# A five-stage graph network kernel: the layers' steps cut into finer pieces and listed in a new order

## The chip, the cores and the metric

The kernel runs on one core of a Trainium2 chip. The time is what the device takes for one execution, in microseconds (us). A core has five engines that run side by side and meet at semaphores: PE multiplies matrices and transposes tiles (its weight loads are shown as PEld), DVE works on vectors and reduces rows, ACT evaluates functions such as Exp and Gelu and copies, POOL does further elementwise work, and SP issues the transfers.

## What is computed

A batch of 16 graphs of 512 nodes with 128 features passes through four layers, each behind a layer norm and a ReLU.

```
h = relu(layernorm(x));  x = x + L0(h, adj)      # eight Euler steps
h = relu(layernorm(x));  x = x + L1(h, adj)      # graph attention: softmax over all neighbours, one head
h = relu(layernorm(x));  x = x + L2(h, src, dst) # attention over 256 edges, four heads
h = relu(layernorm(x));  x = x + L3(h, adj)      # Chebyshev step, 4-head masked attention, MLP
# L3: xp = L_norm @ h; x1 = relu(ln(xp @ Wc + bc)) + h
#     o = softmax(mask(q k^T / sqrt(32))) v;  x2 = ln(x1 + o @ Wo + bo)
#     out = ln(x2 + gelu(x2 @ W1 + b1) @ W2 + b2)
```

## The kernel before

The first part (`build_front`) computes layer L0 and constants; the change doesn't touch it. The second part (`build_layers`) is a software pipeline over the 16 graphs. It has five stages: `gat` (L1), `edge` (L2), `cheb` (the first half of L3 with q, k and v), `att` (the attention of L3) and `ffn` (the rest). In iteration i, stage s works on graph n = i - LAG[s], with lags of 0 to 4, so that five graphs are in flight. There are 20 iterations: 5 that fill, 11 in a hardware loop, 4 that drain.

Each engine has a list of named steps, `ORDER`, and executes it from left to right in each iteration. A step waits at semaphores for what it needs: `ready` for data, `freed` for a buffer that must have been read. An engine never goes past a waiting step, so the lists alone decide what stands behind what.

What the steps are, as far as they matter here. A node tile is 128 rows; four make a graph. Attention has 16 tiles (4 heads by 4 row tiles). In `att{j}`, PE computes the scores of tile j and transposes tile j-2 into bank c2; DVE masks tile j (L1501, `mask j` in what follows); ACT takes its Exp (L1320, `exp j`) and copies the transposed tile out of c2 (L1328). Steps att16 to att18 finish a graph in the next iteration: the last transposes (`turn 14`, `turn 15`), the row sums (`rows`) and the product with v (`pv`), which writes c2. DVE's `att_scale` (L1513) reads c2, and only then PE may transpose the next graph's tile 0 into it (`turn 0`, L1704).

In `gat`, DVE's `gat_scores` adds the mask (L1378), POOL's `gat_low` makes the scaled copy (L1247, four tiles), DVE's `gat_max` takes the larger (L1395, four tiles), ACT's `gat_exp` follows (L1288), and PE's `gat_eturn` transposes (L1597). `gat_stats` (L1110 on gat_xin) waits for `load_x` (L1181 on SP), `gat_apply` (L1145 on gat_z) for POOL's `gat_rstd`, and PE's `gat_turn` (L1558) for gat_z. In `edge`, PE's `edge_gather` (L1614, eight products of 512 columns) writes bank b0. That bank holds the product of `ffn_down` before, which DVE's `ffn_y3` (L1529) must have read. `cheb_prop` (L1664) is twelve products of 512 columns; `n1_apply` (L1145 on cheb_y) and POOL's n1 affine (L1150, L1152 on cheb_y) lead to `cheb_x1`, which PE transposes. `cheb_klow` (L1492 on k_lo) splits k. SP's `stack0` to `stack3` (L1210) move the split q and k of each head into K_parts and Q_parts with 8 transfers of 64 KB each; the scores of head h wait for `parts{h}`.

Of the kernel before, what the change touches and what calls it, by code (L numbers as in the profile page):

```python
# [1779 lines left out]
```

## Time and profile before

| what | value |
|---|---|
| time, median of 3 runs | 1535.29 us (1531.87 to 1538.79) |
| profiled execution: its own time | 1538.55 us |
| profiled execution: span, first to last instruction | 1536.8 us |
| PE busy | 1245.7 us (81%), weight loads 953.8 us (62%) |
| DVE busy | 834.5 us (54%) |
| ACT busy | 772.1 us (50%) |
| POOL busy | 471.6 us (31%) |
| mean granted clock of PE | 0.92 |

Busy time is the time in which an engine has an instruction under way. The span has three parts: L0 up to some 460 us, the pipeline's filling up to some 634 us, then the full iterations and the drain. A granted clock of 1.00 is 2.4 GHz, one of 0.50 is 1.2 GHz.

### The profile page before, as it was taken

What the parts mean: (1) busy time and instruction counts of PE and PEld (TensorE: products, weight loads), DVE (VectorE), ACT (ScalarE), POOL (GpSimd) and SP (SyncE); (2) the same over time, 40 slices, a digit from 0 to 9 for tenths busy, and PEclk for the clock granted to TensorE, in tenths of its full rate; (3) what the DMA queues carried; (4) which work ended last, traced back from release to release, by engine and by line L of the source; (5) the groups of instructions that cost most, each with busy time, mean ns of one, the idle gap of its engine ahead of it and who ended that gap; (6) DMA issues with size and microseconds to landing.
All of it is one profiled execution on the core that took longest, in us unless ns stands there. A gap on an engine that the chain in (4) does not pass through costs nothing. (4 is left out here: it accounts for less than half of the span.)

```text
span 1536.8 us, 24908 instructions
## 1 busy us (share of the span) xinstructions
PE 1245.7 (81%) x7613; PEld 953.8 (62%) x7613; DVE 834.5 (54%) x2837; ACT 772.1 (50%) x1612; POOL 471.6 (31%) x578
## 2 busy tenths in 40 slices
PE   5899999999964576887887988888878878878754
PEld 3578788888953454665665665666656656655432
DVE  6632131322323456677668677677676676755431
ACT  4124233331102226667667667667676676665651
POOL 5012030113402223325245244244343352442222
PEclk8899999999985788999999999999999999999976
DMA  5010111101010012322312412413313224124210
GB/s 101 14 42 8 43 34 35 49 15 48 1 35 7 14 43 54 90 57 66 99 46 63 109 35 74 105 30 84 75 47 96 55 61 103 43 64 101 67 52 12
DMA packets 123742, 83.62 MB, mean 54 GB/s; under 512 B 13216, under 2 KB 106784, under 8 KB 123680
## 3 DMA queue, kind: packets, MB, share of 16 engines
q1 hardware_dynamic: 123680, 82.82, 21.1%
q8 instruction: 35, 0.57, 0.2%
q14 instruction: 27, 0.22, 0.0%
HBM read 28.25 MB, written 20.97 MB: 32 GB/s over the span
## 5 line engine op out<-in xcount | busy, mean ns | idle before, releaser
L1320 ACT ACTIVATE att_Es<-att_Ts,att_small 128x512 f32<-128x512 f32 x256 | 184.0, 719 | 139.3 <-DVE att_small L1501 130.5
L1501 DVE CUSTOM_DVE_ANT_0 att_Ts<-bank,mask_att 128x512 f32<-128x512 f32 x256 | 174.3, 686 | 132.2 <-PE bank L1568 131.0
L1704 PE MATMUL bank<-ident,att_Es 128*128 128x128 f32 x1024 | 168.5, 290 | 81.7 <-ACT att_PTs L1328 69.6
L1704 PEld LDWEIGHTS bank<-ident,att_Es 128*128 128x128 f32 x1024 | 122.2, 147 | 148.0 <-ACT att_Es L1320 91.3
L1328 ACT COPY att_PTs<-bank 128x512 f32<-128x512 f32 x256 | 145.7, 569 | 18.3 <-PE bank L1704 18.1
L1568 PE MATMUL bank<-K_parts,Q_parts 128*128 128x512 f32 x256 | 133.9, 533 | 3.6 <-DVE att_small L1501 3.6
L289 POOL TENSOR_SCALAR l_rs<-l_mv 128x4 f32<-128x4 f32 x16 | 6.9, 432 | 248.4 <-DVE l_mv L469 248.3
L844 PE MATMUL bank<-G,x0T 128*128 128x128 f32 x384 | 75.9, 280 | 1.2 <-DVE U2T L478 1.0
L483 DVE TENSOR_TENSOR P_row<-bank,l_bias 128x512 f32<-128x512 f32 x32 | 22.1, 691 | 99.2 <-PE bank L854 77.7
L844 PE MATMUL bank<-G,U2T 128*128 128x128 f32 x384 | 75.0, 277 | 0.0
L844 PE MATMUL bank<-G,U1T 128*128 128x128 f32 x384 | 75.0, 277 | 0.0
L1597 PE MATMUL bank<-ident,gat_Ts 128*128 128x128 f32 x256 | 42.2, 303 | 39.8 <-ACT gat_Ts L1288 37.7
L1395 DVE TENSOR_TENSOR gat_Vs<-gat_Ts,gat_Vs 128x512 f32<-128x512 f32 x64 | 70.7, 1155 | 4.8 <-POOL gat_Vs L1247 4.8
L1288 ACT ACTIVATE gat_Ts<-gat_Vs,gat_small 128x512 f32<-128x512 f32 x64 | 46.0, 719 | 53.6 <-DVE gat_Vs L1395 53.6
L1150 POOL TENSOR_TENSOR ffn_y3s<-ffn_y3s,rowv 128x512 f32<-128x512 f32 x16 | 20.3, 1270 | 170.4 <-DVE ffn_y3s L1145 170.4
L1568 PEld LDWEIGHTS bank<-K_parts,Q_parts 128*128 128x128 f32 x256 | 50.3, 202 | 27.7 <-issue 21.1
L844 PEld LDWEIGHTS bank<-G,x0T 128*128 128x128 f32 x384 | 61.8, 194 | 5.4 <-issue 2.4
L1127 POOL TENSOR_SCALAR cheb_rs<-cheb_mv 128x4 f32<-128x4 f32 x16 | 3.7, 233 | 199.3 <-DVE cheb_mv L1113 199.3
L1597 PEld LDWEIGHTS bank<-ident,gat_Ts 128*128 128x128 f32 x256 | 31.3, 154 | 51.8 <-ACT gat_Ts L1288 51.7
L1604 PE MATMUL bank<-gat_whs,gat_ETs 128*128 128x128 f32 x512 | 61.5, 279 | 0.7 <-ACT gat_ETs L1295 0.7
L1604 PEld LDWEIGHTS bank<-gat_whs,gat_ETs 128*128 128x128 f32 x512 | 60.2, 196 | 1.2 <-ACT gat_ETs L1295 1.1
L1247 POOL TENSOR_SCALAR gat_Vs<-gat_Ts,gat_small 128x512 f32<-128x512 f32 x64 | 47.1, 752 | 42.9 <-DVE gat_small L1390 42.9
(307 smaller groups left out, 3236.0 us busy)
## 6 DMA issues: line engine op xcount, KB each, us to landing
Q_parts<-q_hi SPq DMA_DIRECT2D x128, 64.0 KB, 2.0
Q_parts<-q_lo SPq DMA_DIRECT2D x128, 64.0 KB, 2.0
K_parts<-k_hi SPq DMA_DIRECT2D x128, 64.0 KB, 2.0
K_parts<-k_lo SPq DMA_DIRECT2D x128, 64.0 KB, 2.0
l_x<-in_x SPq DMA_DIRECT2D x16, 256.0 KB, 3.0
P2T<-in_x SPq DMA_DIRECT2D x16, 256.0 KB, 4.2
x_after_l<-P2T SPq DMA_DIRECT2D x16, 256.0 KB, 2.3
gat_xin<-x_after_l SPq DMA_DIRECT2D x16, 256.0 KB, 3.2
```

Of the source, the lines that this page charges most:

```text
L483: nc.vector.tensor_tensor(by_batch(zs[:, t, :]), by_batch(bank[t][:]), bias[:, BLOCKS - 1 - lev, t:t + 1, :].broadcast_to([P, CB, D]), ALU.add
L844: mm = nc.tensor.matmul(bank[t][:, b * D:(b + 1) * D], UT[i][:, b, cols(t)], G[:, STEPS - k0 - i, :], start=(b == 0 and i == 0), stop=(lev ...
L1247: nc.gpsimd.tensor_scalar(gat_V[:, t, :], gat_T[:, t, :], 0.2, gat_small[:, 5, t:t + 1], ALU.mult, ALU.add).then_inc(sem("gat_low"), 1)
L1288: nc.scalar.activation(gat_E[:, t, :], gat_V[:, t, :], ACT.Exp, bias=gat_small[:, 4, t:t + 1], accum_out=gat_small[:, 6, t:t + 1]).then_in ...
L1320: nc.scalar.activation(att_E[:, j % RING_E, :], att_T[:, j % RING_T, :], ACT.Exp, scale=-1.0, bias=att_small[:, 0, j:j + 1], accum_out=att ...
L1328: nc.scalar.copy(att_PT[:, i // NT, :, cols(i % NT)], c2[:].rearrange("p (s q) -> p s q", q=P)).then_inc(sem("att_pt"), 1)
L1395: nc.vector.tensor_tensor(gat_V[:, t, :], gat_T[:, t, :], gat_V[:, t, :], ALU.max).then_inc(sem("gat_max"), 1)
L1501: nc.vector.tensor_tensor_reduce(att_T[:, j % RING_T, :], [c0, c1][j % 2][:], k.mask_att[:, j % NT, :], -QK_SCALE, HUGE, ALU.add, ALU.min, ...
L1568: return nc.tensor.matmul(dst, left, right, start=True, stop=True)
L1597: mm = nc.tensor.transpose([a0, a1][t % 2][:, cols(s)], gat_E[:, t, cols(s)], k.ident[:])
L1604: mm = nc.tensor.matmul(a0[:, cols(t)], gat_ET[:, s, cols(t)], WhA[:, s, :], start=(s == 0), stop=(s == NT - 1))
L1704: mm = nc.tensor.transpose(c2[:, cols(s)], att_E[:, i % RING_E, cols(s)], k.ident[:])
```

## The change

Steps become finer: `gat_scores`, `gat_max`, `gat_low`, `gat_exp`, `gat_eT` and `gat_eturn` are one step per row tile; `edge_gather`, `cheb_prop`, `gat_pv`, `ffn_down` and `att_pv` are two halves; each layer norm has its statistics (`_stats`), their aggregation (`_aggr`), and its gain and bias (`_g`, `_b`) as steps of their own; `att{j}` becomes `att_score`, `att_mask`, `att_exp`, `att_turn` and `att_copy`. A `+` behind a step's name lists it one iteration later. The instructions and their shapes stay the same; some waits that guard a buffer are added to the new pieces. PE's order is the same except that the step boundaries are finer; transpose 14 now ends its own iteration instead of beginning the next. The number of iterations stays 20 (`FILL` is 5).

```diff
 ORDER = {
...
     "DVE": """
-        cheb_stats att16 edge_stats att0 att1 cheb_lo att_scale att2 gat_stats att3 ffn_y2 gat_apply att4
-        n2_apply cheb_y att5 gat_s1_out att6 gat_scores att7 n1_apply gat_max att8 ffn_y3 cheb_x1 att9 cheb_qlow
...
+        cheb_stats gat_x2b+ cheb_aggr att_mask0 edge_stats att_mask1 edge_aggr gat_stats att_scale att_mask2
+        cheb_lo gat_aggr ffn_y2 att_mask3 n2_stats n2_aggr gat_apply n2_apply att_mask4 cheb_y n1_stats
...
     """.split(),
     "SP": """
-        load_x load_ffn cheb_res load_v stack0 stack2 stack1 stack3 store_out store_v edge_store
+        load_ffn load_x stack1+ stack3+ store_v+ edge_store+ load_v cheb_res stack0 stack2 store_out
     """.split(),
 }
+FILL = 1 + max(LAG[STAGE_OF[step.rstrip("+")]] + step.count("+") for order in ORDER.values() for step in order)
...
-        def run(eng, fori, order, steps, att):
+        def run(eng, fori, order, steps):
+
+            lags = {step: LAG[STAGE_OF[step.rstrip("+")]] + step.count("+") for step in order}
 
             def iteration(i):
                 for step in order:
-                    n = i - LAG[STAGE_OF[step]]
+                    n = i - lags[step]
                     if isinstance(i, int) and not 0 <= n < B:
                         continue
-                    if step in steps:
-                        steps[step](n)
-                    else:
-                        att(n, int(step[3:]))
...
+                    steps[step.rstrip("+")](n)
...
-            def gat_max(n):
-                for t in range(NT):
-                    ready(dve, "gat_low", n, t + 1, NT)
-                    nc.vector.tensor_tensor(gat_V[:, t, :], gat_T[:, t, :], gat_V[:, t, :], ALU.max
-                                            ).then_inc(sem("gat_max"), 1)
...
+            def gat_max(n, t):
+                ready(dve, "gat_low", n, t + 1, NT)
+                nc.vector.tensor_tensor(gat_V[:, t, :], gat_T[:, t, :], gat_V[:, t, :], ALU.max
+                                        ).then_inc(sem("gat_max"), 1)
...
+            def gat_x2(n, t0):
+                if t0 == 0:
+                    ready(dve, "gat_rinv", n)
+                    freed(dve, "edge_done", n)
                 ready(dve, "gat_pv", n)
-                freed(dve, "edge_done", n)
-                for t in range(NT):
+                for t in (t0, t0 + 1):
                     nc.vector.scalar_tensor_tensor(x2[:, t, :], a0[:, cols(t)], gat_small[:, 7, t:t + 1],
                                                    xA[:, t, :], ALU.mult, ALU.add).then_inc(sem("gat_done"), 1)
```

First place: DVE in the loop, from mask 7 to the layer norm's sum `cheb_x1`. Before (`ISA att_Ts` is a mask, `gat_Vs` a `gat_max`, `cheb_y` is `n1_apply`, `ffn_y3s<-bank` is `ffn_y3`):

```order
L1501 ISA att_Ts,att_small<-bank,mask_att 128x512
...
L1145 TENSOR_SCALAR cheb_y<-cheb_y,n_mv,n_rs 128x128 x4
L1395 TENSOR_TENSOR gat_Vs<-gat_Ts,gat_Vs 128x512 x2
...
L1395 TENSOR_TENSOR gat_Vs<-gat_Ts,gat_Vs 128x512 x2
...
L1501 ISA att_Ts,att_small<-bank,mask_att 128x512
...
L1529 TENSOR_TENSOR ffn_y3s<-bank,ffn_y2s 128x512
L1110 BN_STATS n_stat<-ffn_y3s 128x6 x4
...
L1485 SCALAR_TENSOR_TENSOR cheb_x1s<-cheb_y,cheb_hs 128x512
```

The same stretch of the changed kernel, with its own line numbers:

```order
L1545 ISA att_Ts,att_small<-bank,mask_att 128x512
...
L1427 TENSOR_TENSOR gat_Vs<-gat_Ts,gat_Vs 128x512
...
L1427 TENSOR_TENSOR gat_Vs<-gat_Ts,gat_Vs 128x512
L1174 TENSOR_SCALAR cheb_y<-cheb_y,n_mv,n_rs 128x128 x4
L1427 TENSOR_TENSOR gat_Vs<-gat_Ts,gat_Vs 128x512
...
L1545 ISA att_Ts,att_small<-bank,mask_att 128x512
...
L1580 TENSOR_TENSOR ffn_y3s<-bank,ffn_y2s 128x512
L1427 TENSOR_TENSOR gat_Vs<-gat_Ts,gat_Vs 128x512
...
L1532 SCALAR_TENSOR_TENSOR cheb_x1s<-cheb_y,cheb_hs 128x512
```

`n1_apply` has moved from ahead of all four `gat_max` to behind the second, and the fourth `gat_max` stands behind mask 8 and `ffn_y3`.

Second place: DVE at the head of the loop's body, up to the sum of `ffn_y2`. Before (`att_oTs` is `att_scale`, `gat_stat` is `gat_stats`, `h_lo` is `cheb_lo`):

```order
L1110 BN_STATS cheb_stat<-x 128x6 x4
...
L1113 BN_AGGR cheb_mv<-cheb_stat 128x2 x4
...
L1110 BN_STATS edge_stat<-x 128x6 x4
...
L1501 ISA att_Ts,att_small<-bank,mask_att 128x512
...
L1501 ISA att_Ts,att_small<-bank,mask_att 128x512
...
L1468 TENSOR_TENSOR h_lo<-cheb_hs,h_hi 128x512
L1513 TENSOR_TENSOR att_oTs<-bank,att_row_scale 128x512
...
L1501 ISA att_Ts,att_small<-bank,mask_att 128x512
...
L1110 BN_STATS gat_stat<-gat_xin 128x6 x4
...
L1113 BN_AGGR gat_mv<-gat_stat 128x2 x4
...
L1518 TENSOR_TENSOR ffn_y2s<-bank,ffn_xr 128x512
```

And now:

```order
L1135 BN_STATS cheb_stat<-x 128x6 x4
L1441 SCALAR_TENSOR_TENSOR x<-bank,gat_small,gat_xin 128x128 x2
...
L1142 BN_AGGR cheb_mv<-cheb_stat 128x2 x4
...
L1545 ISA att_Ts,att_small<-bank,mask_att 128x512
...
L1135 BN_STATS edge_stat<-x 128x6 x4
...
L1545 ISA att_Ts,att_small<-bank,mask_att 128x512
...
L1135 BN_STATS gat_stat<-gat_xin 128x6 x4
...
L1559 TENSOR_TENSOR att_oTs<-bank,att_row_scale 128x512
...
L1545 ISA att_Ts,att_small<-bank,mask_att 128x512
...
L1510 TENSOR_TENSOR h_lo<-cheb_hs,h_hi 128x512
...
L1142 BN_AGGR gat_mv<-gat_stat 128x2 x4
L1564 TENSOR_TENSOR ffn_y2s<-bank,ffn_xr 128x512
```

The second half of `gat_x2` has come in at the head, and `gat_stats` has moved ahead of `att_scale` and mask 2.

Third place: SP at the head of the loop's body. Before:

```order
L1181 DMA gat_xin<-x_after_l 128x4x128
...
L1216 DMA ffn_xr<-attn_residual 128x4x128
L1219 DMA ffn_x<-x_after_l 128x4x128
...
L1189 DMA attn_residual<-cheb_x1s 128x4x128
...
L1198 DMA v_in<-values 128x4x128
...
L1210 DMA Q_parts<-q_hi 32x512 x2
L1210 DMA Q_parts<-q_lo 32x512 x2
```

And now:

```order
L1245 DMA ffn_xr<-attn_residual 128x4x128
L1248 DMA ffn_x<-x_after_l 128x4x128
...
L1210 DMA gat_xin<-x_after_l 128x4x128
...
L1239 DMA Q_parts<-q_hi 32x512 x2
L1239 DMA Q_parts<-q_lo 32x512 x2
L1239 DMA K_parts<-k_hi 32x512
```

`load_x` is now behind the two loads of `load_ffn`, and `stack1+` and `stack3+` follow (16 transfers that stood at the end of the body); `store_out`, which waits for DVE's last sum, is now the last row of the body.

## Rows read from the trace of the kernel before

**Rows 1.** Stretches of two iterations: us, busy us of PE, PEld, DVE, ACT, POOL, clock.
```profile
931.60:990.50 58.90, 48.95 (x328) 36.11 (x328) 42.99 (x151) 40.19 (x87) 23.71 (x29) 0.97 0.28 71
990.50:1050.80 60.30, 50.11 (x329) 37.14 (x329) 43.06 (x152) 40.19 (x87) 23.68 (x29) 0.94 0.27 70
```

**Rows 2.** Timeline of DVE: `ffn_y3` in iterations 4 and 15.
```profile
663.86 0.68 DVE L1529 TENSOR_TENSOR ffn_y3s<-bank,ffn_y2s 128x512 f32<-128x512 f32 x1
...
1322.73 0.68 DVE L1529 TENSOR_TENSOR ffn_y3s<-bank,ffn_y2s 128x512 f32<-128x512 f32 x1
```

**Rows 3.** Timeline of one iteration ahead of the gather.
```profile
950.77 0.69 DVE L1501 CUSTOM_DVE_ANT_0 att_Ts<-bank,mask_att 128x512 f32<-128x512 f32 x1 [1.19 <-PE bank L1568]
...
954.90 2.71 POOL L1247 TENSOR_SCALAR gat_Vs<-gat_Ts,gat_small 128x512 f32<-128x512 f32 x4 [1.65 <-DVE gat_small L1390]
955.22 2.48 DVE L1145 TENSOR_SCALAR cheb_y<-cheb_y,n_mv,n_rs 128x128 f32<-128x128 f32 x4
...
957.61 4.62 DVE L1395 TENSOR_TENSOR gat_Vs<-gat_Ts,gat_Vs 128x512 f32<-128x512 f32 x4
...
960.86 0.66 PE L1597 MATMUL bank<-ident,gat_Ts 128*128 128x128 f32 x4 [1.01 <-ACT gat_Ts L1288]
...
962.16 0.68 DVE L1501 CUSTOM_DVE_ANT_0 att_Ts<-bank,mask_att 128x512 f32<-128x512 f32 x1
...
963.54 0.77 PE L1614 MATMUL bank<-edge_pick,h_hi 128*128 128x512 f32 x1 [2.03 <-issue]
```

**Rows 4.** Timeline of iteration 0, where `gat_max` and `gat_low` overlap.
```profile
475.05 0.69 DVE L1395 TENSOR_TENSOR gat_Vs<-gat_Ts,gat_Vs 128x512 f32<-128x512 f32 x1 [0.51 <-POOL gat_Vs L1247]
...
473.12 4.31 POOL L1247 TENSOR_SCALAR gat_Vs<-gat_Ts,gat_small 128x512 f32<-128x512 f32 x4 [11.84 <-DVE gat_small L1390]
```

**Rows 5.** Stretches ahead of and in the gather: us, PE busy, granted clock.
```profile
960.03:963.44 3.41, 0.66 (x4) 1.00 0.00 0
963.44:966.85 3.41, 3.31 (x8) 0.50 0.02 6
```

**Rows 6.** Timeline of PE: first and last of `cheb_prop`'s 12 products, last of the gather's 8.
```profile
940.27 0.48 PE L1664 MATMUL bank<-lap_hi,h_hi 128*128 128x512 f32 x1
...
942.92 0.40 PE L1664 MATMUL bank<-lap_hi,h_lo 128*128 128x512 f32 x1
...
966.67 0.48 PE L1614 MATMUL bank<-edge_pick,h_lo 128*128 128x512 f32 x1
```

**Rows 7.** Timeline of the same iteration's head.
```profile
930.54 0.86 DVE L1110 BATCH_NORM_STATS2 cheb_stat<-x 128x6 f32<-128x128 f32 x4
...
936.08 0.40 SPq L1181 DMA_DIRECT2D gat_xin<-x_after_l  x1
...
937.05 0.68 DVE L1513 TENSOR_TENSOR att_oTs<-bank,att_row_scale 128x512 f32<-128x512 f32 x1
...
937.79 0.66 PE L1704 MATMUL bank<-ident,att_Es 128*128 128x128 f32 x4 [0.65 <-DVE att_oTs L1513]
...
939.38 0.87 DVE L1110 BATCH_NORM_STATS2 gat_stat<-gat_xin 128x6 f32<-128x128 f32 x4 [1.03 <-DMA gat_xin<-x_after_l]
...
943.86 1.08 DVE L1145 TENSOR_SCALAR gat_z<-gat_xin,gat_mv,gat_rs 128x128 f32<-128x128 f32 x4
...
944.99 0.66 PE L1558 MATMUL bank<-ident,gat_z 128*128 128x128 f32 x4 [1.01 <-DVE gat_z L1145]
```

**Rows 8.** Timeline of the same iteration: mask 12, transpose 11, scores 0 and 1.
```profile
980.25 0.69 DVE L1501 CUSTOM_DVE_ANT_0 att_Ts<-bank,mask_att 128x512 f32<-128x512 f32 x1 [0.52 <-PE bank L1568]
...
982.42 0.63 PE L1704 MATMUL bank<-ident,att_Es 128*128 128x128 f32 x4 [0.81 <-ACT att_PTs L1328]
...
989.52 0.71 PE L1568 MATMUL bank<-K_parts,Q_parts 128*128 128x512 f32 x2
```

**Rows 9.** The page's DMA issues: KB each, us to landing.
```profile
gat_xin<-x_after_l SPq DMA_DIRECT2D x16, 256.0 KB, 3.2
```

**Rows 10.** The page's costliest groups, ACT's `gat_exp`: busy, mean ns of one, idle before.
```profile
L1288 ACT ACTIVATE gat_Ts<-gat_Vs,gat_small 128x512 f32<-128x512 f32 x64 | 46.0, 719 | 53.6 <-DVE gat_Vs L1395 53.6
```

More of the change, by code:

```diff
@@ L988 @@
     "gat": """
-        load_x gat_rstd gat_stats gat_hT gat_turn gat_apply gat_wh gat_wh_out gat_s2 gat_s1_out gat_scores
-        gat_low gat_exp gat_max gat_eT0 gat_eturn0 gat_eturn2 gat_eT2 gat_pv gat_x2
+        gat_turn gat_wh gat_s1 gat_s2 gat_eturn0 gat_eturn1 gat_eturn2 gat_eturn3 gat_pv0 gat_pv1 gat_stats
+        gat_aggr gat_apply gat_s1_out gat_scores0 gat_scores1 gat_scores2 gat_scores3 gat_row1 gat_row2 gat_row3
+        gat_max0 gat_max1 gat_max2 gat_max3 gat_rinv gat_x2a gat_x2b gat_hT gat_wh_out gat_exp0 gat_exp1
@@ L996 @@
+        edge_x3 edge_apply edge_hi edge_hg edge_xz edge_exp edge_yT edge_rstd edge_lo edge_store
     """.split(),
     "cheb": """
-        cheb_rstd cheb_stats cheb_apply cheb_hi cheb_lo cheb_xpT cheb_res cheb_prop cheb_g stack0 cheb_y
-        stack2 stack1 n1_rstd stack3 n1_apply n1_affine cheb_x1 cheb_x1turn cheb_x1T cheb_q cheb_qsplit
-        cheb_qlow cheb_ksplit cheb_klow cheb_k cheb_vout cheb_v store_v
+        cheb_prop0 cheb_prop1 cheb_g cheb_x1turn cheb_q cheb_k cheb_v cheb_stats cheb_aggr cheb_lo cheb_y
@@ L1003 @@
+    """.split(),
     "ffn": """
-        load_ffn att_scale ffn_res ffn_wo n2_rstd ffn_y2 n2_apply n2_affine ffn_turn ffn_x2T ffn_b2
-        ffn_gelu ffn_up n3_rstd ffn_y3 ffn_down n3_apply store_out n3_affine ffn_final
-    """.split() + [f"att{j}" for j in range(TILES, TILES + 3)],
+        ffn_wo ffn_turn ffn_up0 ffn_up1 ffn_down0 ffn_down1 att_scale ffn_y2 n2_stats n2_aggr n2_apply ffn_y3
+        n3_stats n3_aggr n3_apply ffn_final ffn_x2T ffn_gelu0 ffn_gelu1 ffn_res n2_rstd n2_g n2_b ffn_b2 n3_rstd
+        n3_g n3_b load_ffn store_out
@@ L1007 @@
+    """.split(),
 }
@@ L1634, in edge_lcol, with edge_v @@
                 mm.then_inc(sem("edge_lcol"), 1)
+            def edge_v(n):
+                ready(pe, "edge_max", n, ET * H, ET * H)
                 for e in range(ET):
@@ new lines, in att_rows, with att_pv @@
+            def att_rows(n):
+                ready(pe, "att_rv", n)
+                need(pe, sem("edge_done"), min(n + 3, B) if isinstance(n, int) else n + 3)
+                for t in range(NT):
+                    for h in range(H):
+                        i = h * NT + t
+                        mm = one(b1[HD * h:HD * (h + 1), cols(t)],
+                                 att_small[:, 2, i:i + 1].broadcast_to([P, HD]), k.ident[:])
+                mm.then_inc(sem("att_rows"), 1)
+            def att_pv(n, half):
+                if half == 0:
```

418 lines of the change are left out of this document (234 added, 184 removed).

## The prediction

> **What bounds the kernel now.** I read the busy time by stretches first, cut at the iterations [rows 1]. A full iteration takes 58.9 or 60.3 us, in turn. PE is busy for 49 to 50 us of it, DVE for 43, ACT for 40, POOL for 24. So PE is nearest to being the bound, and what an order can win is at most PE's idle 10 us in each. From one `ffn_y3` to the eleventh after it the pipeline takes 1322.73 - 663.86 = 658.9 us, 59.9 us each [rows 2].
>
> Then the timeline, to see where PE's idle time lies. The largest piece is ahead of `edge_gather` [rows 3]: transpose group 1 of `gat` starts at 960.86 after 1.01 us of waiting, and the gather at 963.54 after 2.03 us more. It needs bank b0, which DVE's `ffn_y3` has to read first; that stands behind mask 8 (962.16). DVE is busy all the time up to there: `n1_apply` takes 2.48 us while POOL runs `gat_low`, then the four `gat_max` take 4.62 us, against 0.69 us for one alone [rows 4], while POOL runs n1's affine. The other pieces of idle time that the change reaches are 0.65 us ahead of turn 0 (for `att_scale`), 1.01 us ahead of `gat_turn` (for gat_z) [rows 7] and 0.81 us ahead of turn 11 [rows 8].
>
> The granted clock comes third [rows 5]. PE, which had 0.66 us of work between 960.03 and 963.44, is granted 0.50 (1.2 GHz) from 963.44 to 966.85, which is just where the gather runs. Its eight products start at 963.54 to 966.67 [rows 3, 6], 3.13 / 7 = 0.45 us apart; the twelve of `cheb_prop`, as wide and at full clock, start 2.65 / 11 = 0.24 us apart [rows 6]. The iteration of 60.3 us has a mean clock of 0.94, the one of 58.9 us has 0.97 [rows 1]: in the long ones the low clock lasts longer, and costs 1.4 us more.
>
> **The change part by part.** PE's own order stays as it was, apart from transpose 14, which ends one body where it began the next: in a loop that is the same place. The instructions are the same ones. What changes is when PE's waits end. All times below are in the frame of the iteration of rows 3, 7 and 8.
>
> *Ahead of the gather.* (a) The first `gat_scores` now stands before mask 6. DVE waits 1.19 us there [rows 3], so its 0.69 us fit into that wait, and everything behind begins about 0.6 us earlier: `gat_low` at 954.3 instead of 954.90. (b) From its end of tile 0 (955.0), DVE now runs two `gat_max`, `n1_apply`, the third `gat_max`, mask 8 and `ffn_y3`. The first two `gat_max` run beside `gat_low`. Iteration 0 shows what that does: they take 0.69 us and 0.51 us pass before the next, since the two engines take turns [rows 4]. So 0.69 + 0.51 + 0.69 = 1.9 us. `n1_apply` then runs beside the last two tiles of `gat_low`. Its price is 1.1 us at least (gat_z, the same shape, took 1.08 [rows 7]) and 2.48 at most [rows 3]; I take 2.3, since half of `gat_low` is still to come. The third `gat_max` is 0.69 us. Mask 8 begins at 955.0 + 1.9 + 2.3 + 0.7 = 959.9 to 960.3, with the small gaps 960.2, and the gather 1.4 us later as it does now (963.54 - 962.16) at 961.6. That is 1.9 us earlier; with `n1_apply` at its lower bound 3.1, at its upper 1.7. (c) PE must be there in time: its transpose group 1 waits for the second `gat_exp`, which ACT can give at about 959.6, so that this group ends near 960.4 and hides nothing of the gain.
>
> One `gat_max` is now behind `ffn_y3`. It will cost up to 1.6 us beside POOL's affine ((4.62 - 2 x 0.69) / 2, if two of the four were slowed [rows 3, 4]), and delays `cheb_x1`. PE has the gather, scores 9 and turn 7 to do before it needs that, some 4.5 us. It stays hidden as long as the gather runs at the low clock, and is just hidden at the full one.
>
> *At the head.* `gat_x2`'s second half, the sum `ffn_final` (0.69 us) and POOL's order move. DVE's last sum would end where `cheb_stats` starts now, plus its own 0.69 us (930.54 + 0.69 = 931.2 [rows 7]), and release SP's `store_out`; with the branch and two loads ahead, SP issues `load_x` at 933.9 instead of 936.08 [rows 7], and it lands 3.2 us later [rows 9], at 937.1. `gat_stats` (0.87 us) is now in front of `att_scale`, so `att_scale` begins at 938.0 instead of 937.05, and turn 0 is 1.0 us late. Queued behind it are mask 2, exp 2 and turn 1. But `gat_stats` itself comes 1.4 us earlier than 939.38, and the 1.01 us that PE waits for gat_z before `gat_turn` go away: gat_z is ready at about 944.2. Loss and gain meet at `gat_turn`: 944.8 instead of 944.99. I count 0 to -0.2, and take -0.2.
>
> *Behind.* `cheb_klow` (0.69 us) moves from before `edge_max` to before mask 12. DVE waits 0.52 us there [rows 8]; the rest, 0.2 us, reaches mask 12, exp 12 and PE's turn 11, which has no slack. +0.2 us. K_parts for head 0 is filled some 6 us later than now, at about 981; scores 0 of the next graph come at 989.52 [rows 8], and a larger transfer lands in 3.2 us [rows 9].
>
> *The clock.* With the gather ahead by 2 us, PE's idle time before it shrinks from 3.0 us in two pieces to about 1.3. In this trace the clock fell at this one place in each full iteration, after PE had done 0.66 us of work in a stretch of 3.41 [rows 5], and not at the other waits of about 1 us [rows 7, 8]. So I expect it to stay at 2.4 GHz in most iterations. Of the 8 x 0.21 = 1.7 us that the gather then saves little reaches the end, since ACT is not ready: from about 958 it has four `gat_exp` (0.72 us each [rows 10]), an exp and three copies of the same width, some 7 us with the gaps, before `edge_hgs` and `cheb_xTs`. What does come is the longer low stretch of every second iteration, 1.4 / 2 = 0.7 us.
>
> The Trainium skill (SBUF — State Buffer, "Who interferes with whom") says that a DVE instruction with two SBUF inputs and a reading POOL instruction exclude each other for a whole instruction, while one with a PSUM input doesn't contend. Rows 4 agree (0.51 us of waiting between `gat_max`). By the page `ffn_y3` and the masks, which read a bank, keep their 0.68 us beside POOL's affine; the sum above is the same by both.
>
> **The sum.** Against a mean full iteration of (58.9 + 60.3) / 2 = 59.6 us: -1.9 - 0.2 + 0.2 - 0.7 = -2.6 us; (a) may bring 0.2 more, as DVE's gaps close. Take -2.7. It applies to iterations 4 to 15, twelve of them: -32 us. In the drain SP's `stack1+` lands about when scores 4 want it, since there is no `cheb_prop` in between: 1 us in each of two iterations, +2. L0 is unchanged. 1538.6 - 30 = 1508.6 for an execution like the profiled one; the median lies 3.3 us under that execution, so 1505 us.
>
> **The rivals.**
> - *Clock and gain in full*: ACT follows more quickly than I think, `n1_apply` takes 1.1 us, and the gather's 1.7 us are kept. Then -3.1 - 0.7 - 1.0 = -4.8 us, twelve times: 1480. For it speaks ACT's 33% of idle time, against it ACT's unbroken list in this stretch. Chance 0.12.
> - *The clock still falls*: the transposes ahead of the gather don't keep it up. Then the 0.7 us are missing, and `gat_max` 3 stays hidden: -1.9 us each, with the drain's +2 in all -21: 1515. Chance 0.25.
> - *It doesn't matter*: the gather comes earlier, but `cheb_x1` (behind the fourth `gat_max` and POOL's affine) or ACT's list gives it back before k is split. Each has under 1 us of slack at full clock. Under 0.6 us stay per iteration: 1530 to 1538. Chance 0.1.
> - *Slower*: `gat_stats` in front of `att_scale`. Its price is 1 us per us by which gat_xin lands after 937.1, and 1 us is given back at `gat_turn`. The point from which it decides is a landing 2.7 us later, at 939.8: as late as it is now (939.38), plus 0.4. It would be reached if SP's `store_out` or `load_ffn` held `load_x` up for 3 us, for `ffn_final` or `ffn_y2` of the graph before. With a landing at 942.5: +2.7 us each, 1567. Against it: DVE's last sum is followed by SP within 0.5 us by the order, and nothing in the rows is that late. Chance 0.05.
> - *Slower by the clock*: the new idle time before turn 0 (1.65 us instead of 0.65 [rows 7]), with 0.66 us of transposes behind it, takes the clock down at `cheb_prop`, whose twelve products then cost 12 x 0.21 = 2.5 us more. With the clock kept at the gather that leaves -0.1 us an iteration, with it lost there too +0.6: 1536 to 1544. Chance 0.06. The Trainium skill (TensorE: Matmul & The Clock Gate, "A second HAM failure mode: psum-queue depth-cycling") says that short idle times between groups of matmuls can make the clock go down and up again; the rows show no such fall at waits of about 1 us.
>
> **How the numbers follow.** The forecast has 0.42. The range leaves out one in ten on each side: from 1482, near the rival in full, to 1530, which takes in the still falling clock and half of the case that doesn't matter. A measurement of this kernel can tell about 0.5%, 7.7 us, from no change. Faster than 1527.6: forecast, full, still falling and a part of the next, 0.82. Within 7.7 us: 0.10. Slower: 0.08.
>
> **What would show it.** Right: `ffn_y3` to `ffn_y3` of 57 us, `n1_apply` between the second and third `gat_max`, the gather's eight products in 2 us instead of 3.6, a mean clock above 0.92, no wait before `gat_turn`, and about 1.6 us before turn 0. Wrong: the gather waits for something else than `ffn_y3`; ACT's wait before `cheb_xTs` or `q_hi` grows by what the gather gained; DVE waits for gat_xin by more than 2 us; the low clock turns up at another place; or scores 4 wait for `parts1`.

## The result and the profile after

The changed kernel takes 1460.03 us (median of 4 runs, 1458.83 to 1461.45), the one before 1537.04 in the same session: ratio 0.9495, 95% interval 0.9452 to 0.9538. I had forecast 1505 and a range of 1482 to 1530. The direction was right, the size about half of what came.

The profiled execution took 1458.87 us, 79.7 less than the one of before (1538.55). The windows tell where. From `ffn_y3` of iteration 4 to that of iteration 15 the kernel before took 658.87 us, and the four iterations behind it, the drain, 203.17 (us, busy us of PE, PEld, DVE, ACT, POOL, clock, DMA share, GB/s):

```profile
663.86:1322.73 658.87, 544.72 (x3608) 402.45 (x3608) 473.32 (x1664) 441.97 (x958) 261.10 (x319) 0.96 0.28 70
1322.73:1525.90 203.17, 147.63 (x887) 99.50 (x887) 92.97 (x340) 111.51 (x236) 55.52 (x61) 0.84 0.25 63
```

The same two stretches after, and one iteration to set beside [rows 1]:

```profile
661.07:1263.70 602.63, 521.96 (x3611) 389.94 (x3612) 434.57 (x1664) 436.55 (x958) 271.48 (x320) 0.99 0.29 77
...
1263.70:1446.19 182.49, 136.50 (x890) 92.45 (x888) 92.06 (x341) 111.40 (x238) 57.52 (x63) 0.93 0.27 68
...
935.74:990.20 54.46, 47.21 (x330) 35.18 (x329) 39.47 (x152) 39.65 (x88) 24.74 (x30) 1.00 0.29 77
```

A full iteration fell from 59.90 to 54.78 us: -5.1, eleven times, is -56.3 of the 79.7. The drain gave -20.7, and the way to the first `ffn_y3` (663.86 [rows 2], 661.07 after) -2.8. PE's busy time fell by 22.8 us in the eleven iterations, with the same work: that is the clock, 0.96 to 0.99. DVE's fell by 38.8 us, 3.5 an iteration. Most of that is `gat_max` (4.85 to 2.74 us an iteration) and `n1_apply` (2.73 to 2.07), which no longer run beside POOL for so long.

DVE's timeline after, ahead of the gather, answers to [rows 3] (start us, us, line, op, in brackets the idle time before and who ended it; L1427 is `gat_max`, L1174 `n1_apply`, L1545 mask 8, L1580 `ffn_y3`, L1532 `cheb_x1`):

```profile
985.43 0.69 DVE L1427 TENSOR_TENSOR gat_Vs<-gat_Ts,gat_Vs 128x512 f32<-128x512 f32 x1 [0.25 <-POOL gat_Vs L1275]
986.64 0.69 DVE L1427 TENSOR_TENSOR gat_Vs<-gat_Ts,gat_Vs 128x512 f32<-128x512 f32 x1 [0.51 <-POOL gat_Vs L1275]
987.25 1.82 DVE L1174 TENSOR_SCALAR cheb_y<-cheb_y,n_mv,n_rs 128x128 f32<-128x128 f32 x4
988.99 0.68 DVE L1427 TENSOR_TENSOR gat_Vs<-gat_Ts,gat_Vs 128x512 f32<-128x512 f32 x1
989.59 0.68 DVE L1545 CUSTOM_DVE_ANT_0 att_Ts<-bank,mask_att 128x512 f32<-128x512 f32 x1
...
990.20 0.68 DVE L1580 TENSOR_TENSOR ffn_y3s<-bank,ffn_y2s 128x512 f32<-128x512 f32 x1
990.80 0.67 DVE L1427 TENSOR_TENSOR gat_Vs<-gat_Ts,gat_Vs 128x512 f32<-128x512 f32 x1
992.78 0.69 DVE L1532 SCALAR_TENSOR_TENSOR cheb_x1s<-cheb_y,cheb_hs 128x512 f32<-128x512 f32 x1 [1.30 <-POOL cheb_y L1183]
```

And PE in the same iteration: turn 0 (the wait that became longer), `gat_turn`, and the gather's first and last product:

```profile
969.42 0.66 PE L1772 MATMUL bank<-ident,att_Es 128*128 128x128 f32 x4 [2.10 <-DVE att_oTs L1559]
...
975.46 0.60 PE L1620 MATMUL bank<-ident,gat_z 128*128 128x128 f32 x4
...
990.98 0.47 PE L1681 MATMUL bank<-edge_pick,h_hi 128*128 128x512 f32 x1 [0.47 <-issue]
...
992.69 0.39 PE L1681 MATMUL bank<-edge_pick,h_lo 128*128 128x512 f32 x1
```

The reader should see three things. The gather's products are (992.69 - 990.98) / 7 = 0.24 us apart instead of 0.45 [rows 3, 6]. PE waits 0.47 us for the gather instead of 2.03 [rows 3]. And turn 0 waits 2.10 us instead of 0.65 [rows 7], while the wait ahead of `gat_turn` is gone.

### The profile page after: what moved, and what is told of

It is laid out like the page before. It is cut to its first block and busy times, and to the rows that moved or that the text cites. A ratio compares the mean times of both kernels' runs of the same rounds, so it can differ in the third digit from the quotient of the medians.

```text
span 1457.1 us, 25026 instructions
## 1 busy us (share of the span) xinstructions
PE 1215.8 (83%) x7613; PEld 937.7 (64%) x7613; DVE 786.6 (54%) x2837; ACT 765.2 (53%) x1612; POOL 484.9 (33%) x578
## 5 line engine op out<-in xcount | busy, mean ns | idle before, releaser
L1772 PE MATMUL bank<-ident,att_Es 128*128 128x128 f32 x1024 | 161.8, 281 | 93.4 <-ACT att_PTs L1348 66.8
L1772 PEld LDWEIGHTS bank<-ident,att_Es 128*128 128x128 f32 x1024 | 119.0, 143 | 154.1 <-ACT att_Es L1340 85.5
L1545 DVE CUSTOM_DVE_ANT_0 att_Ts<-bank,mask_att 128x512 f32<-128x512 f32 x256 | 174.5, 683 | 77.7 <-PE bank L1630 74.1
L1147 POOL TENSOR_SCALAR n_rs<-n_mv 128x4 f32<-128x4 f32 x48 | 12.3, 257 | 204.7 <-DVE n_mv L1142 204.6
L1275 POOL TENSOR_SCALAR gat_Vs<-gat_Ts,gat_small 128x512 f32<-128x512 f32 x64 | 61.5, 975 | 37.4 <-DVE gat_small L1422 37.4
L1630 PEld LDWEIGHTS bank<-K_parts,Q_parts 128*128 128x128 f32 x256 | 48.2, 193 | 27.2 <-issue 22.7
L845 PEld LDWEIGHTS bank<-G,U2T 128*128 128x128 f32 x384 | 59.3, 195 | 0.0
L845 PEld LDWEIGHTS bank<-G,U1T 128*128 128x128 f32 x384 | 59.3, 195 | 0.0
L1792 PE MATMUL bank<-att_PTs,v_in 128*32 128x512 f32 x512 | 57.9, 592 | 0.0
```

The source lines that it names most:

```text
L845: mm = nc.tensor.matmul(bank[t][:, b * D:(b + 1) * D], UT[i][:, b, cols(t)], G[:, STEPS - k0 - i, :], start=(b == 0 and i == 0), stop=(lev ...
L1275: nc.gpsimd.tensor_scalar(gat_V[:, t, :], gat_T[:, t, :], 0.2, gat_small[:, 5, t:t + 1], ALU.mult, ALU.add).then_inc(sem("gat_low"), 1)
L1545: nc.vector.tensor_tensor_reduce(att_T[:, j % RING_T, :], [c0, c1][j % 2][:], k.mask_att[:, j % NT, :], -QK_SCALE, HUGE, ALU.add, ALU.min, ...
L1630: return nc.tensor.matmul(dst, left, right, start=True, stop=True)
L1772: mm = nc.tensor.transpose(c2[:, cols(s)], att_E[:, i % RING_E, cols(s)], k.ident[:])
L1792: mm = nc.tensor.matmul(c2[r, :], vD[:, s, r], att_PT[:, h, s, :], start=(s == 0), stop=(s == NT - 1))
```

## The experiments

Each kernel is the changed code with its lists of order edited (e5 has one more edit, shown there). "Iteration" is the mean from `ffn_y3` of iteration 4 to that of iteration 15 in the run's trace, "drain" the four behind. Both come from the one profiled execution, which lies within 5 us of the median, except in e14: there it is the slowest of four, 1485.85 us. The ratio is against the kernel before, with its 95% interval.

| kernel | median us | ratio | iteration | drain |
|---|---|---|---|---|
| after | 1460.0 | 0.9495 (0.9452 to 0.9538) | 54.78 | 182.5 |
| e1_old_order | 1543.2 | 1.0019 (0.9986 to 1.0051) | 59.93 | 203.4 |
| e2_gather_alone | 1495.4 | 0.9704 (0.9667 to 0.9741) | 56.44 | 200.4 |
| e3_gather_undone | 1514.9 | 0.9826 (0.9784 to 0.9868) | 59.17 | 186.9 |
| e4_old_sp | 1602.8 | 1.0417 (1.0377 to 1.0456) | 64.18 | 208.5 |
| e5_old_more_turns | 1527.4 | 0.9924 (0.9896 to 0.9951) | 58.55 | 201.6 |
| e6_new_sp_alone | 1527.1 | 0.9919 (0.9888 to 0.9949) | 59.19 | 195.1 |
| e10_both | 1442.5 | 0.9370 (0.9326 to 0.9414) | 53.56 | 184.3 |
| e11_gather_and_sp | 1474.1 | 0.9600 (0.9554 to 0.9646) | 55.32 | 191.8 |
| e12_old_sp_stats_behind | 1592.0 | 1.0341 (1.0296 to 1.0385) | 63.13 | 208.5 |
| e13_old_sp_klow_back | 1530.9 | 0.9969 (0.9945 to 0.9992) | 59.04 | 200.8 |
| e14_klow_back | 1474.4 | 0.9579 (0.9529 to 0.9629) | 56.57 | 190.0 |
| e15_both_klow | 1456.0 | 0.9481 (0.9427 to 0.9536) | 54.29 | 189.0 |
| e16_e11_new_rest | 1485.3 | 0.9646 (0.9617 to 0.9675) | 55.72 | 196.7 |
| e17_new_dve_sp | 1476.0 | 0.9591 (0.9555 to 0.9627) | 56.39 | 186.9 |
| e18_e11_klow_late | 1474.6 | 0.9579 (0.9546 to 0.9612) | 55.32 | 193.0 |

### The finer pieces, and the gather's piece alone

e1_old_order has the changed code with every list in the order of before. e2_gather_alone adds one thing, and e3_gather_undone takes that one thing out of the changed kernel:

```diff
 e2: "DVE" of before
-att_mask7 n1_apply gat_max0 gat_max1 gat_max2 gat_max3 att_mask8 ffn_y3 n3_stats
+att_mask7 gat_max0 gat_max1 n1_apply gat_max2 att_mask8 ffn_y3 gat_max3 n3_stats
 e3: "DVE" of after
-att_mask7 gat_max0 gat_max1 n1_apply gat_max2 att_mask8 ffn_y3 gat_max3
+att_mask7 n1_apply gat_max0 gat_max1 gat_max2 gat_max3 att_mask8 ffn_y3
```

> The changed kernel's code (finer pieces, their added waits), with all five lists put back into the old order. Theory A (the order does it: DVE's list ahead of the gather, with the clock that stays up, and SP's list in the drain): as the kernel before, 1537 us, within 8. Rival B (the finer pieces or their waits themselves move the time): off by 10 us or more.

> The old order with one piece of DVE's list new: gat_max 0 and 1, n1_apply, gat_max 2, mask 8, ffn_y3, and gat_max 3 behind ffn_y3. Theory A: the gather comes some 2.5 us earlier, the clock no longer falls at it, and the 1.5 us of its own speed are kept: -4 us in each of 12 iterations, about 1537 - 48 = 1489. The forecast as it was (ACT isn't ready, so the faster gather gives back nothing): -2.6 us each, 1506. Rival C (the gain comes from the other moved steps, on ACT and at the head): above 1520.

> The changed kernel with only that piece of DVE's list put back (n1_apply, gat_max 0 to 3, mask 8, ffn_y3). Theory A: +4 to +5 us in each of 12 iterations, 1460 + 54 = 1514, and the low clock is back at the gather. The forecast as it was: +2.4 us each, 1489. Rival C: below 1475.

Cutting the steps finer does nothing by itself that these runs can tell (59.93 us, and a ratio whose interval takes in 1). The gather's piece is worth 3.5 us an iteration alone, and 59.17 - 54.78 = 4.4 in the changed kernel, where the first `gat_scores` and SP's list are new too. In e2 the low clock shows in one of the eleven iterations (at `gat_turn`), in e3 in each of them at the gather, as before. So the order ahead of the gather decides the fall there, in the old kernel and in the new one.

### Is ACT ready for a faster gather?

e5_old_more_turns keeps every list of before, and lets PE repeat the second group of gat's transposes five times in its idle time ahead of the gather. The extra transposes write what is there already.

```diff
-                for s in range(NT):
+                for s in range(NT * (5 if t == 1 else 1)):
+                    s %= NT
```

> The changed kernel's code with all lists in the order of before; transpose group 1 of gat (four transposes ahead of the gather) is repeated five times, so that PE works for some 1.5 us of its idle time there. No other engine has more to do. Theory (what PE did just before the gather decides the clock there, and ACT has room to follow a faster gather): the granted clock stays at 1.00 at the gather, its products start 0.24 us apart instead of 0.45, and the 1.5 us and the long low stretch of every second iteration come through: 57.5 to 58.3 us from ffn_y3 to ffn_y3 instead of 59.9, 1510 to 1520 us in all, though every wait of DVE and ACT is left as it was. Rival (my prediction: ACT is not ready, a faster gather gives little): 59.2 to 59.9 us, 1530 to 1543 us. If the clock still falls, its fall hangs on something else than PE's work there.

The timeline of PE in this kernel, the twenty transposes and the gather's first and last product, and ahead of them the twenty transposes of an earlier iteration:

```profile
787.51 4.07 PE L1663 MATMUL bank<-ident,gat_Ts 128*128 128x128 f32 x20 [1.01 <-ACT gat_Ts L1313]
...
1023.99 2.40 PE L1663 MATMUL bank<-ident,gat_Ts 128*128 128x128 f32 x20 [1.01 <-ACT gat_Ts L1313]
1026.68 0.47 PE L1682 MATMUL bank<-edge_pick,h_hi 128*128 128x512 f32 x1 [0.28 <-issue]
...
1028.39 0.39 PE L1682 MATMUL bank<-edge_pick,h_lo 128*128 128x512 f32 x1
```

With PE at work up to 0.28 us before the gather, all eleven gathers run at 2.4 GHz. The clock falls twice elsewhere: at 787.65 us under the added transposes themselves, which then take 4.07 us instead of 2.40 and push the gather back, and at 1006.10, in an iteration of 61.6 us. So what PE does ahead of the gather decides the clock in it. The mean is 58.55 us, 1.4 less than e1, with no other engine's list changed. PE's busy time without gat's transposes fell by 1.6 us an iteration (e1: 544.55 - 26.41 = 518.14 us in eleven, e5: 547.15 - 46.74 = 500.41), so most of what PE saves at the higher clock reaches the end. These 1.4 us take in the longer low stretch of every second iteration, for which the forecast had 0.7; by that figure the gather's own part is the other 0.7, or 1.0 when the iteration of 61.6 us is left out (the other ten take 58.25). ACT was not the obstacle that the prediction made of it. The median (1527) lies above the 1510 to 1520 that I expected, for the size.

### SP's list

```diff
 e4 (the changed kernel) and e6 (all else of before), "SP"
-load_ffn load_x stack1+ stack3+ store_v+ edge_store+ load_v cheb_res stack0 stack2 store_out
+load_x load_ffn cheb_res load_v stack0 stack2 stack1 stack3 store_out store_v edge_store
 (e6 the other way round)
```

> The changed kernel with SP's list as before (load_x and load_ffn at the head, all four stacks in their own iteration). Theory A: full iterations within 0.3 us of 54.8, but in the drain load_ffn stands behind four stacks again and ffn_y2 waits for it: +7 to +15 us, 1467 to 1475. Rival D (the drain became shorter by the clock alone): within 3 us of 1460.

> All lists in the order of before, only SP's list is the changed one (load_ffn ahead of load_x, stacks 1 and 3 and the stores of v and of the edge step one iteration late). Theory (what SP's list gives is the drain, where load_ffn stood behind all four stacks): the last four iterations take some 185 to 195 us instead of 203, a full iteration stays within 0.7 us of 59.9: 1520 to 1532 us. Rival (the drain's gain comes from the gather and the clock in the drain, not from SP): drain 200 to 204 us, 1535 to 1543. Second rival (load_x earlier moves the head of each iteration): 59.0 us or less each, and under 1520 in all.

e4 missed by 130 us, and it is the run that taught most. The waits (us in total, times, longest) for the loads that SP issues, before:

```profile
POOL ffn_xr L1252 <- DMA ffn_xr<-attn_residual: 91.5, 16, 18.7
...
DVE gat_stat L1110 <- DMA gat_xin<-x_after_l: 22.9, 15, 6.0
```

after:

```profile
DVE gat_stat L1135 <- DMA gat_xin<-x_after_l: 43.1, 16, 5.4
POOL ffn_xr L1280 <- DMA ffn_xr<-attn_residual: 18.9, 14, 7.1
```

and in e4:

```profile
POOL ffn_xr L1280 <- DMA ffn_xr<-attn_residual: 188.0, 16, 17.8
DVE gat_stat L1135 <- DMA gat_xin<-x_after_l: 148.4, 16, 11.6
```

DVE stands 10.5 to 11.3 us in front of `gat_stats` in each full iteration of e4. I took it for the whole cause, and put `gat_stats` back behind `att_scale` and mask 2, with SP's old list, in e12; e13 puts `cheb_klow` back ahead of `edge_max` as well.

```diff
 e12, e13 "DVE"
-gat_stats att_scale att_mask2 cheb_lo
+att_scale att_mask2 gat_stats cheb_lo
 e13 "DVE"
-edge_z att_mask10 edge_max0 ... edge_le cheb_klow att_mask12
+edge_z att_mask10 cheb_klow edge_max0 ... edge_le att_mask12
```

> As e4 (the changed kernel with SP's list of before, 1603 us), and gat_stats behind att_scale and mask 2 in DVE's list. Theory (e4 was slow because SP, after all four stacks, reaches load_x only at the end of the iteration, and gat_stats ahead of att_scale lets mask, exp and turn wait for it, 10.8 us of DVE's waiting in the one that I read): the wait moves behind masks 0 to 2, most of it is hidden, 56 to 59 us from ffn_y3 to ffn_y3 instead of 64.2, drain some 195 to 205, 1490 to 1540 us. Rival (SP's late list itself holds everything up, through ffn_xr or the K parts): 62 to 64 us each, 1570 to 1603 us.

> As e12 (the changed kernel with SP's old list and gat_stats behind, 1592 us, 63.1 us an iteration), and cheb_klow back in its old place ahead of edge_max. Theory (a loop through SP: the loads at an iteration's start, gat up to the split k, then all of the stacks on SP, 20.6 us from the first K part to load_x, before the next loads; in e12 42.7 us from load_x to the first K part, in before 39.95; k's lateness by some 6 us is what makes it 63): the first K part comes some 6 us sooner, and an iteration takes 56.5 to 58 us, in all 1500 to 1525. Rival (SP's old list is slow by itself with the new order of the others): 61 us or more, over 1560.

e12 fell on its rival's side: 1 us an iteration, not 6. The reason stands in SP's own timeline, here of e12: `load_x`, the first K part (k has just been split), the last K part, and the next `load_x`.

```profile
902.05 0.39 SPq L1210 DMA_DIRECT2D gat_xin<-x_after_l  x1
...
944.71 0.51 SPq L1239 DMA_DIRECT2D K_parts<-k_hi  x1
...
962.24 0.59 SPq L1239 DMA_DIRECT2D K_parts<-k_lo  x1
...
965.28 0.40 SPq L1210 DMA_DIRECT2D gat_xin<-x_after_l  x1
```

There is a loop through SP's queue. Of the 32 transfers of four stacks, four (q of head 0) stand ahead of the first K part. From there SP issues the other 28 back to back, in 962.83 - 944.71 = 18.1 us, then the stores, then `load_x`: 965.28 - 944.71 = 20.57 us. From `load_x` to k's split it takes 944.71 - 902.05 = 42.66. From one `load_x` to the next any two such legs add up to an iteration (63.2 here, 63.13 in the mean), so the sum proves nothing. That the loop binds is seen at its two joints: SP stands idle for 6 us before the first K part, and DVE waits 7.3 to 8.3 us for gat_xin in each full iteration, then 0.95 or more for POOL's `ffn_xr`, whose load stands right behind `load_x` (either load may begin the leg). The test is e13. With `cheb_klow` back, the first K part comes 852.35 - 814.31 = 38.0 us behind `load_x`, the SP leg is 20.6 again, and that iteration is 58.6 us. The mean of 59.04 is 1 us above what I expected, and the clock falls once in each of these iterations; in the one that I read, at `cheb_prop`, for whose `h_lo` behind the late `gat_stats` PE waits 2.5 us. So of e4's excess of 9.4 us an iteration, `cheb_klow`'s late place with SP's full list carries 63.13 - 59.04 = 4.1, `gat_stats` 64.18 - 63.13 = 1.1, and the rest is SP's list with both of them back. With SP's new list, where two stacks stand behind the next `load_x`, `cheb_klow`'s late place costs nothing (e18 below); the place of `gat_stats` was never moved alone there.

The same loop touches e2, too. Its SP timeline has the leg of 20.58, and 35.75 to the first K part, ahead of which SP does not stand idle (it is at work from the first part of q, at 895.46). DVE waits 0.95 to 1.4 us for gat_xin in each full iteration, and PE 1.2 to 1.85 us for gat_z behind it:

```profile
862.33 0.39 SPq L1210 DMA_DIRECT2D gat_xin<-x_after_l  x1
...
898.08 0.51 SPq L1239 DMA_DIRECT2D K_parts<-k_hi  x1
...
918.66 0.40 SPq L1210 DMA_DIRECT2D gat_xin<-x_after_l  x1
```

So SP's list, worth 0.7 us an iteration in the old order (e6), should be worth more once the gather's piece is there. e11 has both.

> All lists in the order of before but for two: SP's list as changed, and DVE's two gat_max ahead of n1_apply (e2 and e6 together). If the two parts simply add, a full iteration takes 59.9 - 3.5 - 0.7 = 55.7 us and the drain 192 to 195, in all 1480 to 1487, and what is left to the changed kernel (54.8 us) is gat_scores before mask 6, and the drain's last 10 us are in the other lists. Rival (SP's list and the gather serve the same loop, so that the second is worth more or less once the first is there): 54.8 or less, or 56.4 as with the gather alone.

55.32 us, which is 1.1 less than e2, and neither wait is left. In e6 they are gone as well, but PE waits 1.46 us ahead of turn 0 there, 0.63 in e1. Whether SP's list wins or saves from a loss depends on what else is in.

The drain's part of SP's list is e6's 203.4 - 195.1 = 8.3 us. There `load_ffn` stood behind all stacks. The timeline before, in the drain:

```profile
1460.91 0.50 SPq L1216 DMA_DIRECT2D ffn_xr<-attn_residual  x1
...
1464.45 1.26 POOL L1252 TENSOR_TENSOR ffn_xr<-ffn_xr,rowv 128x512 f32<-128x512 f32 x1 [18.69 <-DMA ffn_xr<-attn_residual]
1465.81 0.69 DVE L1518 TENSOR_TENSOR ffn_y2s<-bank,ffn_xr 128x512 f32<-128x512 f32 x1 [6.08 <-POOL ffn_xr L1252]
...
1469.87 1.09 PE L1704 MATMUL bank<-ident,att_Es 128*128 128x128 f32 x4 [7.81 <-ACT att_PTs L1328]
```

and after, in the same iteration of the drain (the 15th graph of 16 in both):

```profile
1382.11 0.48 SPq L1245 DMA_DIRECT2D ffn_xr<-attn_residual  x1
...
1387.03 1.27 POOL L1280 TENSOR_TENSOR ffn_xr<-ffn_xr,rowv 128x512 f32<-128x512 f32 x1 [7.10 <-DMA ffn_xr<-attn_residual]
...
1389.69 0.69 DVE L1564 TENSOR_TENSOR ffn_y2s<-bank,ffn_xr 128x512 f32<-128x512 f32 x1 [1.04 <-PE bank L1626]
```

DVE waited 6.08 us for POOL's `ffn_xr`, which waited for the load, and PE 7.81 us for what stood behind it in DVE's order. After, `ffn_y2` waits for PE.

### The head of the iteration, and a faster kernel

e10_both takes the changed kernel, puts `gat_stats` behind `att_scale` and mask 2 as in e12, and `load_x` ahead of `load_ffn`. e14 and e15 put `cheb_klow` ahead of `edge_max` in the changed kernel and in e10.

```diff
 e10, e15 "SP"
-load_ffn load_x stack1+ ...
+load_x load_ffn stack1+ ...
```

> The changed kernel with load_x ahead of load_ffn in SP's list and gat_stats behind att_scale and mask 2 in DVE's. Theory A (the 2.1 us that PE waits ahead of turn 0 for att_scale are given back at gat_turn, since all that lies between has room): turn 0 comes at 6.3 us after turn 15 instead of 7.6, gat_turn at 13.4 to 13.7 as in the changed kernel, a full iteration 54.3 to 54.8, 1450 to 1460 us. Theory B (the wait is a loss, and with gat_xin 0.7 us earlier the late gat_stats costs nothing): gat_turn at 12.6, a full iteration 53.4 to 54.0, 1435 to 1447 us.

> The changed kernel with cheb_klow alone back ahead of edge_max. Theory (with stacks 1 and 3 one iteration late, the K parts have room): 54.6 to 55.0 us an iteration, 1455 to 1465 us; my term for its move was 0.2 us an iteration, the other way. Rival (SP's loop still binds a little): 54.4 or less, under 1453.

> e10 (load_x first, gat_stats behind att_scale and mask 2, 53.6 us an iteration, 1442 us) with cheb_klow back ahead of edge_max. Without slack in turn 11 it may win 0.2 us an iteration (1438 to 1441), or cost 0.2 where edge_max, now later, lets edge_exp wait (1443 to 1447): mostly a second reading of e10.

e10 takes 1442.5 us, the fastest of all, and its interval (0.9326 to 0.9414) lies below the changed kernel's. Turn 0 waits as little as before, and `gat_turn` comes 964.51 - 958.46 = 6.05 us behind it, with no wait, where it was 7.20 before [rows 7]:

```profile
958.46 0.66 PE L1772 MATMUL bank<-ident,att_Es 128*128 128x128 f32 x4 [0.47 <-DVE att_oTs L1559]
...
964.51 0.60 PE L1620 MATMUL bank<-ident,gat_z 128*128 128x128 f32 x4
```

Theory B held: the changed kernel's wait ahead of turn 0 goes with a loss of 1.2 us an iteration, which is not given back at `gat_turn`. What the change gave back there is the old wait of 1.01 us [rows 7], and SP's list alone removes that: in e6, with `gat_stats` in its old place, PE doesn't wait ahead of `gat_turn` in any full iteration. e10 moves `gat_stats` and `load_x` together, so their shares in the 1.2 us are open.

e14 came out slower than both theories allowed, 1474 instead of 1455 to 1465, and its trace, which is of the slowest execution, shows a lower clock. Windows of e14 around turn 0:

```profile
862.00:865.00 3.00, 0.85 (x8) 0.86 (x9) 2.37 (x8) 0.85 (x3) 1.24 (x2) 1.00 0.45 106
865.00:869.50 4.50, 4.50 (x20) 3.69 (x19) 3.94 (x20) 3.82 (x10) 1.89 (x4) 0.62 0.43 100
```

The low clock (0.50) takes the second stretch up to 868.7, where the first four of `cheb_prop`'s products run. This happens in nine of the eleven iterations of e14's trace, with turn 0 waiting 1.96 to 2.69 us in the nine, and in two of the changed kernel's eleven, of 55.2 and 55.8 us where the others take 54.4 to 55.0:

```profile
693.00:695.10 2.10, 0.70 (x6) 0.71 (x7) 2.10 (x8) 0.44 (x3) 0.72 (x2) 0.99 0.42 100
695.10:698.50 3.40, 3.40 (x15) 3.12 (x14) 2.54 (x11) 3.26 (x8) 1.27 (x2) 0.51 0.43 99
```

In e10, whose turn 0 waits 0.47 us, it doesn't happen in the full iterations at all. e15 takes 1456 us, 14 more than e10 and over both of its expectations: 54.29 us an iteration, with falls of the clock in three of them, and 4.7 us more in the drain. Why the clock falls there, at other places than turn 0, I can't say. The Trainium skill (TensorE: Matmul & The Clock Gate, "A second HAM failure mode: psum-queue depth-cycling") says that short idle times between groups of matmuls make the clock swing between its levels; the trace agrees at this place (2.1 us with 0.70 of work, then 1.2 GHz), which the rows of before did not yet show.

### What is left

e11's two pieces give 1474 us, the changed kernel 1460. Three kernels ask where the rest lies: e16 has e11's DVE list and everything else as changed, e17 only DVE's and SP's lists as changed, and e18 is e11 with `cheb_klow` late.

```diff
 e18 "DVE" of e11
-edge_z cheb_klow edge_max0 ... edge_le att_mask12
+edge_z edge_max0 ... edge_le cheb_klow att_mask12
```

> PE's, ACT's, POOL's and SP's lists as changed, DVE's in the order of before with the gather piece. If the drain's last 9 us lie in ACT's and PE's lists (att_copy14, copy15 and the spread, now at the end of their own iteration), the drain takes 183 to 186 us here and 190 to 192 in e17, in all about 1463 to 1470. If they lie in DVE's, it stays at 190 to 192, and 1470 to 1478 in all.

> DVE's and SP's lists as changed, PE's, ACT's and POOL's in the order of before. If DVE's list has the last 9 us of the drain, 182 to 185 us there and 1455 to 1465 in all; if not, 190 to 192, and 1465 to 1475.

> e11 (gather piece and SP's list, 55.3 us an iteration, 1474 us) with cheb_klow moved to just ahead of mask 12, nothing else. By my term +0.2 us an iteration: 55.5, 1474 to 1480. By e14's sign, without its falls of the clock, -0.3 to -0.8 us: 54.5 to 55.0, 1462 to 1470.

e18 settles `cheb_klow` against both of its expectations: 55.32 us with and without, so its move costs and wins nothing here. That leaves the falls of the clock as what differs in e14; that they cause its loss, and what causes them, no run tried apart. e16 and e17 don't split the rest. Each is slower than e11 per iteration (55.72 and 56.39, both with falls of the clock around turn 0, which waits 2.0 and 2.24 us there), and only the two together reach 54.78. In the drain e17 takes 186.9, e16 196.7, both together 182.5: DVE's list seems to have about half of the last 9 us, and which of its steps stays open.

## Why the prediction was right and where it was wrong

The forecast was a sum of -30 us. The profiled run has -79.7: 26.6 us more in the eleven full iterations (5.1 instead of 2.7), and 22.7 more in the drain. The way to the first `ffn_y3` came as forecast, and that is luck: in the other kernels this `ffn_y3` begins anywhere from 655 to 676 us, in e1, with every list of before, at 668.3. Of the 2.4 us that an iteration gained beyond the forecast, the readings below give 1.0 to the order ahead of the gather and about 1.4 to the clock (PE's busy time fell by 22.8 / 11 = 2.07 us, where the sum had 0.7); the head and SP's list are smaller and their parts not separated.

- *(a) the earlier `gat_scores`*, -0.6: `gat_low` starts 984.71 - 975.46 = 9.25 us behind `gat_turn`, 9.91 before [rows 3, 7]. Right (-0.66).
- *(b) the order of `gat_max` and `n1_apply`*: right in kind, small in size. I had mask 8 come 5.9 us behind the start of `gat_low` instead of 7.26 [rows 3]; it came 989.59 - 984.71 = 4.88 behind. `n1_apply` took 1.82 us, not 2.3, and DVE's instructions of 0.69 us begin 0.60 apart, where I counted 0.69 and small gaps. 1.0 us an iteration.
- *The deferred `gat_max`* "will cost up to 1.6 us beside POOL's affine": it took 0.67. Unneeded caution; it began at 990.80, POOL's next step on cheb_y only at 990.88, and that one took 1.77 us, against 1.28 for POOL's instruction of the same form at 982.05. The Trainium skill's rule (SBUF — State Buffer, "Who interferes with whom") that the two engines exclude each other for a whole instruction fits: DVE was first, and POOL's took 0.5 us longer.
- *The clock*: right that the fall at the gather goes away. **Wrong step: "Of the 8 x 0.21 = 1.7 us that the gather then saves little reaches the end, since ACT is not ready."** e5 shows that the clock alone is worth 1.4 us an iteration, not 0.7, out of 1.6 that PE saves there. ACT's list from exp 7 to copy 6 takes 4.5 us for seven instructions, where I had some 7 for eight:

```profile
987.10 0.72 ACT L1340 ACTIVATE att_Es<-att_Ts,att_small 128x512 f32<-128x512 f32 x1
...
988.28 0.72 ACT L1313 ACTIVATE gat_Ts<-gat_Vs,gat_small 128x512 f32<-128x512 f32 x1
988.91 0.19 ACT L1313 ACTIVATION_READ_ACCUMULATOR gat_Ts<-gat_Vs,gat_small 128x1 f32 x1
989.00 0.71 ACT L1313 ACTIVATE gat_Ts<-gat_Vs,gat_small 128x512 f32<-128x512 f32 x1
...
991.60 0.72 ACT L1313 ACTIVATE gat_Ts<-gat_Vs,gat_small 128x512 f32<-128x512 f32 x1
```

  The accumulator's read of 0.19 us begins before its exp has ended and overlaps the next: 989.00 - 988.28 = 0.72 us from one `gat_exp` to the next, so it adds nothing. I had this case as a rival at 0.12; it should have been the forecast. Its price had a slip as well: with the gather's 1.7 us kept in full, as its words say, the sum is -3.1 - 0.7 - 1.7 = -5.5 us and 1471, not -4.8 and 1480.
- *The head*, -0.2: `gat_xin` landed later than I had it (4.0 us behind its issue by the page of after, 3.2 [rows 9]), and DVE waited 2.85 us for it. Its place in front of `att_scale` cost 1.4 us at turn 0 instead of 1.0, and `gat_turn` came 0.25 later behind turn 15 than before. e10 shows that the order at this place, with SP's, loses 1.2 us an iteration against a better one.

```profile
967.90 0.87 DVE L1135 BATCH_NORM_STATS2 gat_stat<-gat_xin 128x6 f32<-128x128 f32 x4 [2.85 <-DMA gat_xin<-x_after_l]
```

- *`cheb_klow`*, +0.2: measured 0 (e18, in the order of e11).
- *SP's list*: I had no term for it in the full iterations, and measured 0.7 (e6) to 1.1 us (e11 against e2).
- **Wrong step: the drain, "+2".** I looked at what the late stacks would cost scores 4, and not at what the four stacks held up behind them: -8.3 us (e6). The rest, 12.4 us, goes with a clock of 0.93 instead of 0.84 in the drain and PE's busy time down by 11.1 us (4.5 of them in e6 already, 150.10 to 145.65), and how it divides stays open.
- *The rival "slower by `gat_stats`"*, 1567 at 2.7 us of lateness: it did not come. e4 shows its condition, `load_x` late behind SP's queue, and 1603 us. But only 1.1 of the 9.4 us an iteration are the place of `gat_stats` (e12), so the price was under-rated for another reason: the loop through SP was not seen. *"Slower by the clock" at `cheb_prop`* came in two of eleven iterations. So two of my signs of being wrong were there, the wait for gat_xin over 2 us and a low clock at another place, in a kernel that was faster than forecast.

## What to carry to other kernels

Read the DMA-issuing queue as an engine of its own. Where it issues back to back up to a load that opens the next iteration, it can close a loop. The loop binds where the queue waits for data at one end and an engine for the load at the other, and then the iteration shrinks by what either leg loses: the same list is worth 0.7 us, 1.1 us or, taken away, 9 us an iteration, by what the other engines do. Count what stands behind a queue's long group, not only what the group feeds. And when a change removes a fall of the clock, look for a concrete instruction on each other engine that couldn't follow before the saving is written off: starts in the trace, not sums of durations, tell how fast an engine runs its list.
